# Cross attention: the sixteen columns of score maxima of a head group turned in one transpose to 16 rows of 128, instead of four transposes to 4 rows of 512

## What is computed

```python
q = _split_heads(Q @ Wq.T + bq)          # Q = layernorm(x), 8 batches x 16 heads x 512 x 16
k = _split_heads(K @ Wk.T + bk)          # K = V = ctx_1024
v = _split_heads(V @ Wv.T + bv)
scores = jnp.einsum('bhqd,bhkd->bhqk', q, k) / jnp.sqrt(jnp.float32(D_K))
scores = jnp.where(mask[:, None, :, :] == 0, NEG_INF, scores)
attn = jax.nn.softmax(scores, axis=-1)
out = jnp.einsum('bhqk,bhkd->bhqd', attn, v)
```

## Time and profile before

| | |
|---|---|
| median of three runs | 2753.31 us |
| the profiled execution | 2755.81 us |
| its span in the profile | 2754.1 us |
| cross attention, main loop of 8 batches | about 1097 to 1760 us of the span |
| PE busy over the span | 2213.0 us, 80% |
| DVE busy | 1623.1 us, 59% |
| ACT busy, POOL busy | 912.9 us, 913.8 us, 33% each |
| mean granted TensorE clock | 0.942 of full speed |

### The profile page before, as it was taken

The page is one execution under the profiler, slowest core; times in us unless marked ns, Lnnn a source line. Parts: engine busy times, 40 slices in busy tenths (PEclk is TensorE's granted clock), DMA queues, the critical chain, the costliest instruction groups (busy, mean ns, idle before and its releaser), DMA issues. The chain is left out here.

```text
span 2754.1 us, 37523 instructions
## 1 busy us (share of the span) xinstructions
PE 2213.0 (80%) x11991; PEld 1495.9 (54%) x12000; DVE 1623.1 (59%) x2734; ACT 912.9 (33%) x1265; POOL 913.8 (33%) x778
## 2 busy tenths in 40 slices
PE   2430999999999106989899999756999999999998
PEld 1330999999999102444444444453554555555554
DVE  7720455445554453778777778653666666566565
ACT  2410333433333000445544445321233333233332
POOL 0076455424450631233322333200323323333232
PEclk9999999999999556999999999859999999999998
DMA  3252332333322316465565565523333233223322
GB/s 122 91 215 96 115 118 67 120 119 122 107 73 76 118 55 116 71 108 97 89 96 93 97 108 98 90 73 81 74 77 77 62 77 84 66 66 84 77 54 61
DMA packets 150695, 254.24 MB, mean 92 GB/s; under 512 B 19318, under 2 KB 68350, under 8 KB 148322
## 3 DMA queue, kind: packets, MB, share of 16 engines
q1 hardware_dynamic: 110858, 173.08, 28.9%
q0 software_dynamic: 11104, 44.06, 4.7%
q10 hardware_dynamic: 28688, 36.53, 4.1%
HBM read 130.05 MB, written 67.04 MB: 72 GB/s over the span
## 5 line engine op out<-in xcount | busy, mean ns | idle before, releaser
L1084 DVE TENSOR_REDUCE ca_negmax<-ca_na 128x1 f32<-128x512 f32 x544 | 353.3, 676 | 135.7 <-PE ca_na L874 133.2
L997 ACT ACTIVATE ca_pr<-ca_st 128x1024 f32<-128x1024 f32 x256 | 261.2, 1024 | 290.8 <-PE ca_st L888 290.6
L874 PE MATMUL ca_na<-ca_k_stack,ca_q_stack 128*128 128x512 f32 x544 | 241.8, 450 | 54.2 <-DMA ca_q_stack<-ca_zrow 37.0
L592 DVE TENSOR_TENSOR ex_h<-ex_up,ex_sg 128x512 f32<-128x512 f32 x136 | 94.1, 692 | 305.5 <-ACT ex_sg L555 197.8
L888 PE MATMUL ca_st<-ca_q_stack,ca_k_stack 128*128 128x512 f32 x512 | 269.6, 527 | 0.0
L1688 DVE TENSOR_REDUCE sa_negmax<-sa_na 128x1 f32<-128x512 f32 x272 | 182.6, 674 | 131.1 <-PE sa_na L1509 127.0
L515 PE MATMUL ex_gp<-ex_xp,moe_gu_p 128*128 128x256 f32 x1632 | 221.8, 286 | 1.5 <-DVE ex_xp L578 1.4
L528 PE MATMUL ex_yp<-moe_dn_p,ex_hp 128*128 128x256 f32 x1632 | 209.0, 286 | 11.9 <-DVE ex_hp L582 11.9
L515 PE MATMUL ex_up<-ex_xp,moe_gu_p 128*128 128x256 f32 x1632 | 218.5, 283 | 0.0
L1676 POOL TENSOR_TENSOR sa_acc<-sa_acc,sa_pr 128x1024 f32<-128x1024 f32 x64 | 151.4, 2365 | 170.4 <-ACT sa_pr L1627 170.4
L528 PEld LDWEIGHTS ex_yp<-moe_dn_p,ex_hp 128*128 128x128 f32 x1632 | 198.8, 191 | 15.9 <-DVE ex_hp L582 15.9
(11 more groups left out here) (258 smaller groups left out, 4191.2 us busy)
## 6 DMA issues: line engine op xcount, KB each, us to landing
ca_q_stack<-q_parts SPq DMA_DIRECT2D x144, 128.0 KB
ca_k_stack<-k_parts SPq DMA_DIRECT2D x144, 128.0 KB
sa_q<-sa_qh SPq DMA_DIRECT2D x140, 128.0 KB
sa_k<-sa_kh SPq DMA_DIRECT2D x140, 128.0 KB
ex_raw_m<-masks ACTq DMA_DIRECT2D x34, 512.0 KB, 3.7
moe_gu_raw<-gateupT POOLq DMA_DIRECT2D x8, 2048.0 KB, 8.2
expert_rows<-rt_zeros SPq DMA_DIRECT2D x20, 512.0 KB, 15.7
k_parts<-ca_kp SPq DMA_DIRECT2D x9, 1024.0 KB, 7.3
```

Source lines behind the costliest of these rows:

```text
L592: dve.tensor_tensor(h[:, 2 * q:2 * q + 2, :], up[q % 2][:, :, :], sg[:, q % 2, :, :], ALU.mult).then_inc(h_ready, 1)
L874: pe.matmul(na[s % 2][:, :], q_stack[g][:, h, t * P:(t + 1) * P], k_stack[g][:, h, :], start=not masked, stop=True).then_inc(na_full, 1)
L997: act.activation(pr[:, pair // 2 % 2, h:h + 2, :], st[pair % 2][:, :, :], ACT.Exp, scale=DK ** -0.5).then_inc(exp_done, 1)
L1084: dve.tensor_reduce(negmax[:, g % 2, s % TB, s // TB:s // TB + 1], na[s % 2][:, :], AX.X, ALU.max, negate=True).then_inc(max_done, 1)
```

## The change

`negmax` holds its columns in the order head, query block in place of query block, head. One transpose takes all 16 columns and delivers 16 rows of 128: row 4h + t is the 128 maxima of head h and query block t. `mfull` and `mrow` have that shape, and so have the copy, the split and the source of the DMA; the DMA's destination, one partition of `q_stack`, is written in 16 pieces of 128 numbers. The order of the instructions on each engine is as before, except that three of the four transposes are no longer there.

```diff
-        negmax = m.sb("negmax", [P, 2, TB, HG])
+        negmax = m.sb("negmax", [P, 2, HG, TB])
-        mfull, mrow = m.sb("mfull", [HG, S]), m.sb("mrow", [HG, 2, S], F32R)
+        mfull, mrow = m.sb("mfull", [HG * TB, P]), m.sb("mrow", [HG * TB, 2, P], F32R)
...
                 pe.wait_ge(max_done, a * SLOTS + SLOTS + 2)
-                for t in range(TB):
-                    last = pe.transpose(misc[0:HG, t * P:(t + 1) * P], negmax[:, par, t, :], ident[:, :])
-                last.then_inc(misc_full, 1)
+                pe.transpose(misc[0:HG * TB, 0:P], negmax[:, par, :, :].rearrange("p h t -> p (h t)"), ident[:, :]).then_inc(misc_full, 1)
...
-                    act.copy(mfull[:, :], misc[0:HG, :]).then_inc(misc_free, 1)
+                    act.copy(mfull[:, :], misc[0:HG * TB, 0:P]).then_inc(misc_free, 1)
...
-                    act.dma_start(q_stack[g][R4 + r:R4 + r + 1, :, :].bitcast(F32), mrow[:, r, :].bitcast(F32)).then_inc(m_in, 16)
+                    act.dma_start(q_stack[g][R4 + r:R4 + r + 1, :, :].bitcast(F32).rearrange("a h (t n) -> a (h t) n", n=P), mrow[:, r, :].bitcast(F32)).then_inc(m_in, 16)
...
-                pool.tensor_tensor(mrow[:, 0, :].rearrange("p (t n) -> p t n", n=P), mfull[:, :].rearrange("p (t n) -> p t n", n=P),
-                                   ones[0:HG, :].rearrange("p (a n) -> p a n", a=1).to_broadcast([HG, TB, P]), ALU.mult).then_inc(mh_ready, 1)
+                pool.tensor_tensor(mrow[:, 0, :], mfull[:, :], ones[0:HG * TB, :], ALU.mult).then_inc(mh_ready, 1)
                 pool.wait_ge(mh_ready, a + 1)
                 pool.tensor_tensor(mrow[:, 1, :], mfull[:, :], mrow[:, 0, :].bitcast(F32), ALU.subtract).then_inc(ml_ready, 1)
...
-                dve.tensor_reduce(negmax[:, g % 2, s % TB, s // TB:s // TB + 1], na[s % 2][:, :], AX.X, ALU.max,
+                dve.tensor_reduce(negmax[:, g % 2, s // TB, s % TB:s % TB + 1], na[s % 2][:, :], AX.X, ALU.max,
```

## The result

The changed kernel took 2742.92 us (median of nine runs, 2737.66 to 2744.90), the kernel before beside it 2752.84 us (2746.02 to 2757.47). The ratio is 0.9964, with a 95% interval from 0.9953 to 0.9974: 9.9 us faster. I had forecast 5.3 us, 2748.0, with a range that began at 2743.5. So the direction is right, the size is not, and the measured time lies 0.6 us outside the range. The profiled execution took 2742.50 us with a span of 2740.8; before's took 2755.81 (the table ahead), so the two traces are 13.3 us apart, more than the medians.

The account below looks back on a forecast made before the run. TensorE was taken as busy 80% of the span, bounded in the loop by its waits and, in places, VectorE's pace. Savings of 8 x 0.33 + 8 x 0.32 + 0.1 = 5.3 us off 2753.31 gave 2748.0 us, range 2743.5 to 2754.0.

Parts of the forecast that it names:

- The price of a transpose, 0.11 us: TensorE, full clock: each further transpose in a row costs 0.11 us, so three less save 0.33 us.
- Group 1 gains in full, the wait keeps its length: TensorE's arrival and the stack's landing both move 0.33 us forward; the 3.46 us wait for the stack's load stays.
- Group 2 at half the low-clock price, 0.32 us: Transposes behind the stack wait save 0.63 us at low clock; the stretch ends at the same time, leaving 0.32.
- Groups 3 and 0 gain nothing: The 0.33 us saved there become a longer TensorE wait for VectorE's maximum: nothing gained.
- Only three kinds count: TensorE's loop waits that count: stack's load 26.7 us, VectorE's maximum 11.5 us, mask transfer seven times 1.1 us.
- Rival A: Two or three more batches get the long low-clock stretch, taking back 2.4 to 3.7 us: say 2750.6; chance 0.27.
- I take zero: Maxima's transfers in smaller pieces: disturbing the query store less could give up to 0.1 us a batch, 0.8 in all; counted zero.
- The sum: Loop's eight batches: 8 x 0.33 + 8 x 0.32 = 5.2 us, plus 0.1 for the first batch's group 0: 5.3 us.
- Rival B: Low-clock transposes give 0.63 us each and the store lands 0.1 us sooner: 8.5 us, 2744.8; chance 0.22.
- 0.55 on no measurable change: Chance given to a result within 0.2%, 5.5 us, of the kernel before; faster had 0.39, slower 0.06.

Follow-up runs that it names:

- the one edit meant to bring them back: Changed kernel with the destination of the maxima's transfers written as 4 rows of 512 again: 2740.16 us, 0.9964 of the kernel before.
- The three comparisons: Changed kernel, unedited, timed three times against the kernel before: ratios 0.9964, 0.9977 and 0.9972, together 0.9971 (0.9966 to 0.9977).
- before_again: The kernel before, unchanged, timed and profiled again against itself: 2750.50 us against 2749.17, ratio 1.0007.

## Why the prediction was wrong in size

- **The price of a transpose, 0.11 us:** right. 33 instructions in place of 132, and 8.10, 8.43 and 9.09 us from group 1's transposes to the store with one, four and ten of them: 0.33 for three, 0.99 for nine.
- **Group 1 gains in full, the wait keeps its length:** right, 0.33 us in every batch. With ten transposes the wait stayed at 3.3 us.
- **Group 2 at half the low-clock price, 0.32 us:** right in kind; three transposes measured some 0.24 us and nine 0.9. The 15 us, by which the low clock would count in full, are excluded.
- **Groups 3 and 0 gain nothing:** right, 14.82 us before and after, and 11.5 us of waiting for VectorE became 16.7. The expectation for ten transposes underrated the cover: by the median they cost 3.6 and not 9.6 us.
- **"Only three kinds count":** incomplete. TensorE also waited eight times for `kp`, 5.6 us, and eight times for `qf`, 3.6 us. Both stay (5.8 and 3.6), so it did no harm.
- **Rival A, the low clock moves (the first step that failed):** the sum put the clock at nothing, and the rival priced a change of the long stretches only as a loss of 2.4 to 3.7 us. The profiles of before have a long stretch in the first batch, and one of them a second; the three of the kernel after have none. That is 1.1 us gained in the first batch. I had no reason for a sign and took the bad one. (Rival A's lower time is also wrong by 1 us: 2748.0 + 2.4 is 2750.4.)
- **"I take zero" for the transfers (the second):** I bounded the term at 0.1 us a batch by the share of bytes (1.6% of the store) and left it out. The store became 0.19 us shorter, twice the bound: 1.5 us in eight batches at most. That this reached the end of the chain is not shown, since store and load together did not get shorter. The short packets of 4 bytes, four a transfer before and 16 after, agree with the Trainium skill's rule on the number of engines (DMA: Bandwidth & Descriptors, "Why a DMA increments its semaphore by 16 and not by 1") for these two kernels. That the fewer engines are what held up the store was not tested: the one edit meant to bring them back did not.
- **The sum:** 8 x 0.33 + 8 x 0.24 + 1.1 = 5.7 us is what the timelines of the loop show, so the 5.3 of the forecast hold there, partly by luck: a clock that was left out fills what group 2 lacked. The three comparisons give about 8 us (6.4 to 9.4). Of the 2 us between, up to 1.5 could be the store's, and none is shown. Their cause stays open. The further 1.9 us of the first comparison may be scatter: its nine runs of the kernel before spread over 11 us.
- **The range and the chances:** the range reached 4.5 us below the forecast and missed by 0.6. Rival B, with 0.22, named 8.5 us and is nearest to the measured size, but not for its reason: the full low-clock price that carried it is excluded. 0.55 on no measurable change rested on the forecast lying at the line of 5.5 us.

## What to carry to other kernels

Ask for each engine's saving whether it comes ahead of a chain that ends in the wait, or into another engine's cover: the same three transposes were paid in full in one place, for some 0.24 us in a second and not at all in two others. Small transfers under way beside a large one can lengthen it by more than their share of the bytes (16 KB beside 1 MB: 0.24 us of 4.62), and whether the chain passes that on has to be read at its end and not at the store. And where a wait is followed by a stretch at the low clock, removing the wait can pay for both: here 5 us a batch for an exchange of two jobs, five times what the change itself gained.

## What was not expected

- VectorE's instructions in the combine stage were issued 1.40 us apart for some 30 us in the first profile, each recorded as waiting only for the one ahead of it, and one behind the other at 0.41 us a piece in the second profile of the same program. In the 7 profiles of 16 that have such a stretch the stage's last row shown above, the reciprocal, starts at 1004.6 to 1009.6 us of the span, in the nine others at 998.6 to 1001.2.
- The landing of one and the same load of 1 MB (first issue to the end of the wait) took from 10.95 to 12.2 us within one profile of the kernel before (before_again). That alone is 1 us a batch of scatter, more than what the change saves in one.
- The first transpose behind the wait does not always run at the low clock: in the kernel after, second batch, it took 0.27 us, and the values' matmuls behind it 1.94 us for eight, against 1.06 in that batch of the kernel before. The low stretch began later after the wait and lay on other work.
